# A new layout of the pairs in an interaction network: 11 loads a chunk, x1 sent early, all second-layer tiles in single precision

## The chip, the cores and the metric

One Trainium2 chip, and one of its cores. The metric is the device time of the whole program in microseconds (us), the median of several runs.

## The reference

A recommendation model over 1024 samples. Each looks up 32 rows of 64 numbers, one from each of 32 tables. Two interaction layers follow, both with 128 outputs, and then a small network with relu.

```python
def cin_layer(h, h0, W, b):              # h: [b, Hn, 64], h0: [b, 32, 64]
    Wr = W.reshape(128, Hn, 32)
    x = einsum('bhd,bmd,ohm->bod', h, h0, Wr) + b[None, :, None]
    return relu(x)
x1 = cin_layer(h0, h0, W1, b1)           # h0: the 32 rows
direct2 = cin_layer(x1[:, :64], h0, W2, b2)
z = sum(concat([x1[:, 64:], direct2], axis=1), axis=-1)
y = relu(relu(concat([z, dense_ctx]) @ W_top1 + b_top1) @ W_top2 + b_top2) @ W_top3
```

Layer 1 works on 32 x 32 pairs of rows, which are symmetric; layer 2 on 64 x 32 = 2048 pairs, 16 tiles of 128.

## The kernel before

A chunk is 8 samples, so N = 512 columns; there are 128 chunks in 64 pairs of chunks. Every tile has 128 partitions (pairs of rows) and 512 columns.

**GpSimd** looks up a pair of chunks at a time (L205) and stores the rows feature by feature into a table in HBM, `emb_rows`, with the first 16 features once more behind the 32 (L213), so that reads can wrap.

**SyncE** issues all loads, each 256 KB: `h0` (each feature four times), four `h0shift` tiles (features i+4k to i+4k+3), four `h0rep` tiles for layer 2 (L257), and, from x1 in SBUF, four `x1rep` tiles (L263), each of which spreads 8 partitions of x1 over 128. That is 13 a chunk. Two small loads per pair of chunks bring what layer 1 has left over, `rem_a` and `rem_b`. Its order for chunk c: h0 and shifts of c+2, the x1rep of c+1 as soon as its x1 is there, the h0rep of c+2.

**VectorE** forms the products. Layer 1: `prod1` (L375), 128x2048, with the four-fold h0 as the other factor, and the remainder (L371, L380). Layer 2: two instructions (L403) of 128x4096 for 16 tiles. Half of these tiles are split: ScalarE rounds them to `prod2hi` (L541), VectorE forms the rest, `prod2lo` (L410).

**TensorE** multiplies and adds up in PSUM. A tile in single precision is one matmul in the code and two instructions in the profile. A split tile is three fast matmuls (L472, L473, L479). Its order for chunk c: layer 1 of c+1 (L447, L448), eight tiles of layer 2 in single precision (L465), then the split ones, of which one in every second chunk stays single (L475).

**ScalarE** applies relu and sums over 64 columns, in eight pieces of 64 columns per layer and chunk (L519), each an ACTIVATE and a read of the accumulator. The pieces of layer 1 write all of x1, and the last one releases the fan-out:

```python
if not (last and s == 1):
    act.wait_ge(acc1_ready, c + 2)
    reduce_relu(acc1[1 - s], bias1, x1[1 - s], z1, c + 1, x1_ready)
product_hi(1)
```

All engines run the same `software_pipeline`: two steps by hand, a loop over pairs of chunks, two steps by hand. s is the buffer, the chunk's parity. The top network is run at the end.

Of the kernel before, what the change touches and what calls it, by code (L numbers as in the profile page):

```python
# [14 lines left out]

# [20 lines left out]

def build_dlrm(nc, a):
# [7 lines left out]
    with ctx:  # L47
# [9 lines left out]

        emb = nc.dram_tensor("emb_rows", [WRAP, ROW], fp32, kind="Internal")

# [5 lines left out]
        gathered = sb("gathered", [P, PAIR_GATHERS, D])  # L65
        w1T = sb("w1T", [P, K1, O])
        w1remT = sb("w1remT", [3 * REM, 2, O], fp32r)
        w2T = sb("w2T", [P, len(PLAIN) * NJ, O])
        w2full = sb("w2full", [P, O])
        w2hi = sb("w2hi", [P, len(SPLIT) * NJ, O], fp32r)  # L70
        w2lo = sb("w2lo", [P, len(SPLIT) * NJ, O], fp32r)
        w16hi = sb("w16hi", [P, HALF], fp32r)
        bias1 = sb("bias1", [P, 1])
        bias2 = sb("bias2", [P, 1])
        ident = sb("ident", [P, P])
        h0 = [sb(f"h0_{s}", [P, N]) for s in range(2)]
        h0shift = [sb(f"h0shift_{s}", [P, K1, N]) for s in range(2)]
# [4 lines left out]
        prod1 = [sb(f"prod1_{s}", [P, K1, N]) for s in range(2)]  # L82
        x1 = [sb(f"x1_{s}", [P, N]) for s in range(2)]
        x1rep = [sb(f"x1rep_{s}", [P, NI, N]) for s in range(2)]
        h0rep = [sb(f"h0rep_{s}", [P, NJ, N]) for s in range(2)]
        prod2 = [sb(f"prod2_{n}", [P, 2, NJ, N]) for n in range(2)]
        prod2hi = [sb(f"prod2hi_{n}", [P, NJ, N], fp32r) for n in range(len(SPLIT))]
        prod2lo = [sb(f"prod2lo_{n}", [P, NJ, N], fp32r) for n in range(len(SPLIT))]
# [3 lines left out]
        denseT = sb("denseT", [DENSE, B])  # L92
# [6 lines left out]

        hid1 = [prod2[h][:, 0, :, :] for h in range(2)]  # L100
        hid2 = [prod1[h] for h in range(2)]
# [6 lines left out]

        w1_in = sem("w1_in")
        weights_in = sem("weights_in")  # L110
# [8 lines left out]
        wt1a_zero = sem("wt1a_zero")  # L119
        ident_zero = sem("ident_zero")  # L120
        ident_ready = sem("ident_ready")
        w1_folded = sem("w1_folded")
        w2_grouped = sem("w2_grouped")
        weight_step = sem("weight_step")
        tp_filled = sem("tp_filled")
        tp_copied = sem("tp_copied")
        h0_in = [sem(f"h0_in_{s}") for s in range(2)]
        h0rep_in = [sem(f"h0rep_in_{s}") for s in range(2)]
# [4 lines left out]
        prod1_ready = sem("prod1_ready")  # L133
        prod2_ready = sem("prod2_ready")
        hi_ready = sem("hi_ready")
        lo_ready = sem("lo_ready")
        split_used = sem("split_used")
        acc1_ready = sem("acc1_ready")
        x1_ready = sem("x1_ready")
        z2_ready = sem("z2_ready")  # L140
# [7 lines left out]
        WEIGHT_DMAS = 11  # L148
        STORES = 16 * 2


        w1n = x1rep[0][:, 0:2, :].rearrange("o a n -> o (a n)")
        w2n = x1rep[1][:, :, :].rearrange("o a n -> o (a n)")
        w1fold = x1rep[0][:, 2, :]
        w16 = x1rep[0][:, 3, 0:HALF]
        w1rem = [x1rep[0][:, 3, P * (s + 1):P * (s + 1) + 3 * REM] for s in range(2)]
        w2r = prod2[0][:, 0, :, :].rearrange("o i (j hm) -> o i j hm", j=NJ)

        def four(t):
            return t.rearrange("p k o -> p (k o)")

        turns1 = [([w1fold[:, k * P:(k + 1) * P] for k in range(K1)], P, [(0, K1 * P, four(w1T[:, :, :]), None)]),
                  (w1rem, 3 * REM, [(0, 2 * P, four(w1remT[:, :, :]), None)])]
        turns2 = [([w2r[:, i, j, :] for j in range(NJ)], P,
                   [(0, NJ * P, four(w2T[:, NJ * n:NJ * (n + 1), :]), None)]) for n, i in enumerate(PLAIN)]
        for n, i in enumerate(SPLIT):
            k = NJ * n
            parts = [(0, NJ * P, four(w2hi[:, k:k + NJ, :]), four(w2lo[:, k:k + NJ, :]))]  # L170
            if n == len(SPLIT) - 1:
                parts.append(((NJ - 1) * P, NJ * P, w2full[:, :], None))
            turns2.append(([w2r[:, i, j, :] for j in range(NJ)], P, parts))
        turns2 += [([dense_n[:, 4 * h + t, :] for t in range(4)], DENSE,
                    [(0, N, denseT[:, h * N:(h + 1) * N], None)]) for h in range(2)]
# [14 lines left out]
        def _(pool):  # L190
            nc.gpsimd.memset(wt1a[0:H, :], 0.0).then_inc(wt1a_zero, 1)
# [3 lines left out]
                                    base=0, pattern=[[-1, P]], channel_multiplier=1).then_inc(ident_ready, 1)  # L195
            pool.wait_ge(idx_all_ready, 1)


            with pool.Fori(0, PAIRS) as pair:

# [10 lines left out]
                for f0, nf in ((0, F), (F, WRAP - F)):  # L211
                    dst = bass.AP(emb, f0 * ROW + at, [[ROW, nf], [PAIR_GATHERS * D, GS], [1, PAIR_GATHERS * D]])
                    pool.dma_start(dst, gathered[0:nf * GS, :, :]).then_inc(emb_stored, 16)  # L213

# [3 lines left out]
        def _(sp):  # L218

# [4 lines left out]
            sp.dma_start(w2n, a["L0_rec_W2"]).then_inc(weights_in, 16)  # L224
            sp.dma_start(bias1[:, :], a["L0_rec_b1"].rearrange("(p one) -> p one", one=1)).then_inc(weights_in, 16)
            sp.dma_start(bias2[:, :], a["L0_rec_b2"].rearrange("(p one) -> p one", one=1)).then_inc(weights_in, 16)
            sp.dma_start(dense_n[:, :, :], a["dense_ctx"].rearrange("(t p) c -> p t c", p=P)).then_inc(weights_in, 16)

            sp.dma_start(wt1a[H:P, :], a["W_top1"][0:O - H, :]).then_inc(weights_in, 16)
            sp.dma_start(wt1b[:, :], a["W_top1"][O - H:2 * O - H, :]).then_inc(weights_in, 16)  # L230
            sp.wait_ge(wt1a_zero, 1)
            sp.dma_start(wt1a[0:DENSE, :], a["W_top1"][2 * O - H:2 * O - H + DENSE, :]).then_inc(weights_in, 16)
            sp.dma_start(wt2[:, :, :], a["W_top2"].rearrange("(k p) n -> p k n", p=P)).then_inc(weights_in, 16)
            with nc.allow_non_contiguous_dma(reason="short columns of biases"):
                sp.dma_start(wt3[:, :], a["W_top3"].rearrange("(k p) one -> p (k one)", p=P)).then_inc(weights_in, 16)
                sp.dma_start(bt1[:, :], a["b_top1"].rearrange("(k p) -> p k", p=P)).then_inc(weights_in, 16)
                sp.dma_start(bt2[:, :], a["b_top2"].rearrange("(k p) -> p k", p=P)).then_inc(weights_in, 16)

            def load_h0(col, s):


                sp.dma_start(h0[s][:, :], bass.AP(emb, col, [[ROW, F], [0, SH], [1, N]])).then_inc(h0_in[s], 16)
                for k in range(K1):
                    src = bass.AP(emb, SH * k * ROW + col, [[ROW, F], [ROW, SH], [1, N]])
                    sp.dma_start(h0shift[s][:, k, :], src).then_inc(h0_in[s], 16)

            def load_rem(col):

# [4 lines left out]
            def load_h0rep(col, s):  # L253

                for j in range(NJ):
                    src = bass.AP(emb, GM * j * ROW + col, [[0, GH], [ROW, GM], [1, N]])
                    sp.dma_start(h0rep[s][:, j, :], src).then_inc(h0rep_in[s], 16)  # L257

            def replicate_x1(s):

                for i in range(NI):
                    src = x1[s][GH * i:GH * (i + 1), :].unsqueeze(1).to_broadcast([GH, GM, N])
                    sp.dma_start(x1rep[s][:, i, :], src).then_inc(x1rep_in[s], 16)  # L263
# [3 lines left out]
            load_h0(0, 0)  # L267
            load_h0(N, 1)
            load_h0rep(0, 0)
            sp.wait_ge(x1_ready, 1)  # L270
            replicate_x1(0)
            load_h0rep(N, 1)

            def step(c, pair, s, first, last):
                if not last and s == 0:

                    sp.wait_ge(emb_stored, STORES * pair + 2 * STORES)
                if first and s == 0:
                    sp.wait_ge(prod1_ready, 1)
                else:  # L280


                    sp.wait_ge(prod2_ready, 2 * c)
                if not last:
                    load_h0((c + 2) * N, s)
# [310 lines left out]
```

## Time and profile before

| what | us |
|---|---|
| time, median of 3 runs | 2406.58 |
| fastest and slowest run | 2399.23, 2408.59 |
| span of the profiled execution | 2406.1 |
| TensorE busy in it | 2185.9 |
| VectorE busy | 2029.2 |
| ScalarE busy | 1176.8 |
| data moved by DMA | 468.52 MB, 195 GB/s |

The profile records one execution. Busy time is the union of an engine's instructions; the ends of matmuls are modelled, so they overlap in the records. The chain that ended last is followed back from the last instruction, at each step to what released it.

### The profile page before, as it was taken

The numbers are of one execution on the slowest core, as the hardware profiler recorded it, in microseconds if no ns is written. First come the engines' busy times: TensorE is split into PE (matmuls) and PEld (weight loads), VectorE is DVE, ScalarE is ACT, GpSimd is POOL, SyncE is SP. The second block draws the span as 40 slices with busy tenths as digits, with TensorE's granted clock in tenths as the row PEclk, the third lists the DMA queues.
The fourth block names the chain that finished last, engine by engine and source line by source line (L and its number), as shares of the span: only waits on it lengthen the run. The fifth ranks groups of instructions, "written<-read, shape, count | busy, mean of one in ns | idle before, by whom it ended". The sixth has DMA issues, their size and how long they took to land.

```text
span 2406.1 us, 27920 instructions
## 1 busy us (share of the span) xinstructions
PE 2185.9 (91%) x6314; PEld 1173.3 (49%) x6314; DVE 2029.2 (84%) x828; ACT 1176.8 (49%) x4496; POOL 559.8 (23%) x455
## 2 busy tenths in 40 slices
PE   4999998989999999999999999999999999999998
PEld 2544444445445445445445445445445445445444
DVE  5888888888888888888888888888888888888882
ACT  1455444544554554554554554554554554554553
POOL 4544544455445445444100000000000000000000
PEclk8999999999999999999999999999999999999999
DMA  6788787778878878888877777777777777777760
GB/s 187 207 214 209 200 208 209 205 200 210 220 195 207 213 210 204 215 213 205 211 189 188 201 189 188 201 189 188 202 188 188 199 191 188 200 190 188 198 168 18
DMA packets 262777, 468.52 MB, mean 195 GB/s; under 512 B 37473, under 2 KB 37985, under 8 KB 262642
## 3 DMA queue, kind: packets, MB, share of 16 engines
q1 hardware_dynamic: 249458, 447.44, 72.6%
q0 software_dynamic: 13312, 21.00, 3.3%
q8 instruction: 3, 0.05, 0.0%
q14 instruction: 4, 0.03, 0.0%
HBM read 321.49 MB, written 12.59 MB: 139 GB/s over the span
## 4 chain that ended last, share of the span: by engine, by line
DMA 29%; DVE 25%; SPq 15%; issue 13%; ACT 12%; PE 4%; ACTq 1%; DVEq 0%; POOL 0%; POOLq 0%
DMA x1rep<-x 29%; DVE prod L403 23%; SPq L263 15%; ACT x L519 11%; ACTq L519 1%; PE acc L465 1%; DVE prod L375 1%; DVE prod2lo L410 1%; PE acc L479 0%; PE acc L472 0%; PE acc L473 0%; PE tp L503 0%; PE acc L503 0%; DVEq L402 0%; ACT prod2hi L541 0%
## 5 line engine op out<-in xcount | busy, mean ns | idle before, releaser
L403 DVE TENSOR_TENSOR prod<-h0rep,x1rep 128x4096 f32<-128x4096 f32 x256 | 1121.3, 4421 | 323.5 <-DMA x1rep<-x 293.4
L465 PE MATMUL acc<-prod,w2T 128*128 128x512 f32 x2048 | 950.9, 607 | 196.3 <-DVE prod L403 196.3
L465 PEld LDWEIGHTS acc<-prod,w2T 128*128 128x128 f32 x2048 | 369.7, 190 | 752.1 <-issue 377.1
L519 ACT ACTIVATE acc<-acc,bias 128x64 f32<-128x64 f32 x1024 | 296.1, 294 | 736.8 <-PE acc L479 584.9
L541 ACT CAST prod2hi<-prod 128x2048 fp32r<-128x2048 f32 (+1 forms) x256 | 459.6, 1795 | 248.2 <-DVE prod L403 241.2
L410 DVE TENSOR_TENSOR prod2lo<-prod,prod2hi 128x2048 fp32r<-128x2048 f32 (+1 forms) x256 | 540.0, 2150 | 0.0
L447 PE MATMUL acc<-prod,w1T 128*128 128x512 f32 x1024 | 462.4, 594 | 6.9 <-DVE prod L375 6.9
L472 PE MATMUL acc<-prod2hi,w2lo 128*128 128x512 f32 x960 | 430.9, 449 | 0.0
L205 POOL DMA_INDIRECT gathered<-in_tables,idx x256 | 402.5, 1572 | 112.4 <-issue 58.5
L473 PE MATMUL acc<-prod2hi,w2hi 128*128 128x512 f32 x960 | 378.2, 394 | 0.0
L519 ACT ACTIVATE x<-acc,bias 128x64 f32<-128x64 f32 x1024 | 305.1, 323 | 10.4 <-PE acc L448 10.4
L375 DVE TENSOR_TENSOR prod<-h0shift,h 128x2048 f32<-128x2048 f32 x128 | 291.6, 2278 | 3.5 <-DMA h0shift<-emb_rows 3.5
L447 PEld LDWEIGHTS acc<-prod,w1T 128*128 128x128 f32 x1024 | 194.6, 190 | 203.9 <-issue 192.9
L479 PE MATMUL acc<-prod2lo,w2hi 128*128 128x512 f32 x960 | 290.0, 421 | 0.0
L519 ACT ACTIVATION_READ_ACCUMULATOR x<-acc,bias (+1 forms) x1024 | 220.4, 215 | 0.0
L519 ACT ACTIVATION_READ_ACCUMULATOR acc<-acc,bias (+1 forms) x1024 | 218.3, 213 | 0.8
L472 PEld LDWEIGHTS acc<-prod2hi,w2lo 128*128 128x128 f32 x960 | 180.9, 188 | 68.2 <-issue 30.6
L479 PEld LDWEIGHTS acc<-prod2lo,w2hi 128*128 128x128 f32 x960 | 180.7, 188 | 67.6 <-issue 30.7
L473 PEld LDWEIGHTS acc<-prod2hi,w2hi 128*128 128x128 f32 x960 | 180.8, 188 | 66.8 <-issue 30.6
L525 ACT CAST rem_parts<-rem_prod 32x512 fp32r<-32x512 f32 x64 | 39.7, 621 | 210.0 <-DVE rem_prod L371 188.3
L213 POOL DMA_DIRECT2D emb_rows<-gathered x128 | 73.3, 576 | 283.0 <-DMA gathered<-in_tables,idx 282.9
L201 POOL COPY idx<-idx_all 128x4 int32 x64 | 82.8, 1294 | 213.3 <-DMA emb_rows<-gathered 209.2
(61 smaller groups left out, 430.7 us busy)
## 6 DMA issues: line engine op xcount, KB each, us to landing
h0shift<-emb_rows SPq DMA_DIRECT2D x512, 256.0 KB, 4.5
h0rep<-emb_rows SPq DMA_DIRECT2D x512, 256.0 KB
x1rep<-x SPq DMA_DIRECT2D x512, 256.0 KB
h<-emb_rows SPq DMA_DIRECT2D x128, 256.0 KB, 4.5
emb_rows<-gathered POOLq DMA_DIRECT2D x64, 128.0 KB, 3.0
gathered<-in_tables,idx POOLq DMA_INDIRECT x256
emb_rows<-gathered POOLq DMA_DIRECT2D x64, 64.0 KB, 3.2
rem_a<-emb_rows SPq DMA_DIRECT2D x64, 64.0 KB
```

Source lines behind the costliest of these rows:

```text
L205: nc.gpsimd.indirect_dma_start(out=gathered[:, g, :], out_offset=None, in_=a["tables"], in_offset=bass.IndirectOffsetOnAxis(ap=idx[:, g:g ...
L263: sp.dma_start(x1rep[s][:, i, :], src).then_inc(x1rep_in[s], 16)
L375: return nc.vector.tensor_tensor(prod1[s][:, :, :], h0shift[s][:, :, :], h0[s][:, :].unsqueeze(1).to_broadcast([P, K1, N]), ALU.mult)
L403: nc.vector.tensor_tensor(prod2[n][:, :, :, :], h0rep[s][:, :, :].unsqueeze(1).to_broadcast([P, 2, NJ, N]), x1rep[s][:, 2 * n:2 * n + 2, : ...
L410: nc.vector.tensor_tensor(prod2lo[n][:, 0:m, :], prod2[n][:, 1, 0:m, :], prod2hi[n][:, 0:m, :].bitcast(fp32), ALU.subtract).then_inc(lo_re ...
L447: nc.tensor.matmul(acc1[s][:, :], w1T[:, k, :], prod1[s][:, k, :], start=(k == 0), stop=False)
L465: nc.tensor.matmul(acc2[s][:, :], w2T[:, NJ * n + j, :], prod2[n][:, 0, j, :], start=(n == 0 and j == 0), stop=False)
L472: nc.tensor.matmul(acc2[s][:, :], w2lo[:, k, :], prod2hi[n][:, j, :], start=False, stop=False)
L473: nc.tensor.matmul(acc2[s][:, :], w2hi[:, k, :], prod2hi[n][:, j, :], start=False, stop=False)
L479: mm = nc.tensor.matmul(acc2[s][:, :], w2hi[:, k, :], prod2lo[n][:, j, :], start=False, stop=(n == 1 and j == m - 1))
L519: ins = nc.scalar.activation(out[:, cols], acc[:, cols], ACT.Relu, bias=bias[:, :], accum_out=z[:, bass.ds(c * CB + b, 1)])
L541: nc.scalar.copy(prod2hi[n][:, 0:m, :], prod2[n][:, 1, 0:m, :]).then_inc(hi_ready, 1)
```

## The change

The 2048 pairs of layer 2 are laid out as those of layer 1: a tile has x1 row i (of 32) beside features i+4k to i+4k+3, for two halves of x1 and k from 0 to 7. So the four `h0shift` tiles of layer 1, now called `near`, serve k = 0 to 3 of layer 2 as well, and four `far` tiles bring k = 4 to 7. `x1rep` has two tiles, each spreading 32 partitions of x1 over 128. A chunk has 1 + 4 + 4 + 2 = 11 loads. The stored table repeats all 32 features.

No tile is split: rounding on ScalarE and the difference on VectorE are gone, and so are the fast matmuls of layer 2. ScalarE first writes the 64 rows of x1 that layer 2 needs, in one instruction without sums, and releases the fan-out; the sums of the other 64 rows come later. `prod1` has one buffer instead of two, and so has each half of the layer-2 products. TensorE's order becomes near half, layer 1 of the next chunk, far half. The weights are brought into the new order with wide copies, and the top network's weights are loaded after the first fan-out.

```diff
             def step(c, pair, s, first, last):      # TensorE
-                if not (last and s == 1):
-                    pe.wait_ge(prod1_ready, c + 2)
-                    if not (first and s == 0):
-                        pe.wait_ge(x1_ready, c)
-                    layer1(1 - s)
                 if not first:
                     pe.wait_ge(z2_ready, c - 1)
-                for n in range(2):
-                    pe.wait_ge(prod2_ready, 2 * c + (n + 1))
...
+                layer2_near(c, s)
+                if not (last and s == 1):
+                    pe.wait_ge(p1_ready, c + 2)
+                    if not (first and s == 0):
+                        pe.wait_ge(z1_ready, c)
+                    layer1(1 - s)
+                pe.wait_ge(pfar_ready, c + 1)
+                layer2_far(s)
```

```diff
             def step(c, pair, s, first, last):      # VectorE
...
+                begun = not (first and s == 0)
+                dve.wait_ge(x1rep_in[s], 16 * A2 * pair + 16 * A2)
+                if begun:
+                    dve.wait_ge(pnear_used, c)
+                products2(pnear[:, :, :, :], near[s][:, :, :], s, K1).then_inc(pnear_ready, 1)
+                dve.wait_ge(far_in[s], 16 * K2 * pair + 16 * K2)
+                if begun:
+                    dve.wait_ge(acc2_ready, c)
+                products2(pfar[:, :, :, :], far[s][:, :, :], s, K2).then_inc(pfar_ready, 1)
+                if not last:
+                    if s == 0:
+                        remainder_products(pair + 1)
+                    dve.wait_ge(acc1_ready, c + 2)
+                    done = products1(pair + 1, s)
+                    if s == 0:
+                        done = remainder_lo(pair + 1)
+                    done.then_inc(p1_ready, 1)
```

```diff
             def step(c, pair, s, first, last):      # ScalarE
...
+                if not (last and s == 1):
+                    act.wait_ge(acc1_ready, c + 2)
+                    if begun:
+
+                        act.wait_ge(x1rep_in[1 - s], 16 * A2 * (pair + s))
+                    hidden1(1 - s)
+                if begun:
+                    direct2(c - 1, 1 - s)
+                if s == 0 and not last:
+                    remainder_hi(pair + 1)
+                if not (last and s == 1):
+                    direct1(c + 1, 1 - s)
```

```diff
             def step(c, pair, s, first, last):      # SyncE
...
+                    sp.wait_ge(pnear_ready, c + 1)
+                    load_near((c + 2) * N, s)
+                    if s == 0:
+                        load_rem((c + 2) * N)
+                if not (last and s == 1):
+
+                    sp.wait_ge(x1_ready, c + 2)
+                    if not (first and s == 0):
+                        sp.wait_ge(pfar_ready, c)
+                    replicate_x1(1 - s)
+                if not last:
+                    sp.wait_ge(pfar_ready, c + 1)
+                    load_far((c + 2) * N, s)
```

`layer2_near` and `layer2_far` are eight single-precision matmuls each into the same accumulator; `hidden1` is the one relu of 64 rows, `direct1` and `direct2` are the relus with sums.

## Rows read from the trace of the kernel before

**Rows 1.** Page, engines: busy us, share, instructions.
```profile
PE 2185.9 (91%) x6314; PEld 1173.3 (49%) x6314; DVE 2029.2 (84%) x828; ACT 1176.8 (49%) x4496; POOL 559.8 (23%) x455
```

**Rows 2.** Page, chain that ended last, shares by engine.
```profile
DMA 29%; DVE 25%; SPq 15%; issue 13%; ACT 12%; PE 4%; ACTq 1%; DVEq 0%; POOL 0%; POOLq 0%
```

**Rows 3.** Chain in order of time, one chunk: start us, us, what.
```profile
1228.90 5.87 DMA x1rep<-x
...
1234.97 4.44 DVE prod L403
```

**Rows 4.** Windows: stretch, busy of engines, PEclk, DMA share, GB/s.
```profile
1217.00:1224.00 7.00, 6.28 (x16) 2.61 (x15) 7.00 (x2) 5.09 (x23) 0.00 (x0) 1.00 0.97 301
...
1227.00:1229.00 2.00, 2.00 (x7) 0.91 (x5) 2.00 (x2) 0.19 (x1) 0.00 (x0) 1.00 0.91 101
1229.50:1231.50 2.00, 2.00 (x10) 1.62 (x9) 2.00 (x3) 1.24 (x2) 0.00 (x0) 1.00 0.90 210
...
1218.05:1236.10 18.05, 16.69 (x49) 8.90 (x48) 16.11 (x8) 9.34 (x36) 0.00 (x0) 1.00 0.77 198
2354.40:2358.40 4.00, 0.03 (x1) 0.06 (x1) 4.00 (x2) 2.62 (x17) 0.00 (x0) 1.00 0.00 0
2358.60:2361.90 3.30, 3.30 (x5) 1.22 (x5) 3.30 (x1) 1.56 (x1) 0.00 (x0) 0.50 0.00 0
```

**Rows 5.** Chain in order of time, last chunk and top network.
```profile
2342.37 2.47 ACT x L519 x16
...
2344.90 0.57 SPq L263
...
2348.11 5.61 DMA x1rep<-x
...
2358.37 8.80 PE acc L465 x16
...
2372.74 0.86 PE acc L495 x2
...
2386.48 6.87 PE acc L503 x16
```

**Rows 6.** Timeline of one chunk: start us, us, engine, line, form, count.
```profile
1215.92 1.09 PE L479 MATMUL acc<-prod2lo,w2hi 128*128 128x512 f32 x4
...
1216.84 3.60 PE L447 MATMUL acc<-prod,w1T 128*128 128x512 f32 x8
...
1217.15 0.29 ACT L519 ACTIVATE acc<-acc,bias 128x64 f32<-128x64 f32 x1 [7.54 <-PE acc L479]
...
1219.88 0.80 PE L448 MATMUL acc<-rem_parts,w1remT 96*128 96x512 f32 x1
...
1230.08 2.27 DVE L375 TENSOR_TENSOR prod<-h0shift,h 128x2048 f32<-128x2048 f32 x1
1230.18 0.62 ACT L525 CAST rem_parts<-rem_prod 32x512 fp32r<-32x512 f32 x1 [2.99 <-DVE rem_prod L371]
...
1232.37 0.68 DVE L380 TENSOR_TENSOR rem_parts<-rem_prod,rem_parts 32x512 fp32r<-32x512 f32 x1
```

**Rows 7.** Line 567, top layers' relu: duration ns min/median/max.
```profile
L567 ACT ACTIVATE prod<-acc,bt x6: 687/688/722, 2375.1 to 2393.4; 128x512 f32<-128x512 f32 x6
```

**Rows 8.** DMA issues by line: KB each, us to landing.
```profile
x1rep<-in_L_rec_W SPq DMA_DIRECT2D x1, 512.0 KB, 3.7
...
table_row<-in_table_rows SPq DMA_DIRECT2D x1, 0.5 KB, 2.4
```

**Rows 9.** Chain in order of time, while gathers run.
```profile
316.26 6.25 DMA x1rep<-x
```

**Rows 10.** Timeline of the start.
```profile
29.61 5.89 PE L447 MATMUL acc<-prod,w1T 128*128 128x512 f32 x8 [6.90 <-DVE prod L375]
...
38.28 5.36 SPq L263 DMA_DIRECT2D x1rep<-x  x4
...
52.74 7.58 PE L465 MATMUL acc<-prod,w2T 128*128 128x512 f32 x11 [13.35 <-DVE prod L403]
```

More of the change, by code:

```diff
@@ L81, in build_dlrm @@
         rem_parts = sb("rem_parts", [3 * REM, N], fp32r)
[L82 to L88, printed above, removed]
+        prod1 = sb("prod1", [P, K1, N])
+        x1 = [sb(f"x1_{s}", [H, N]) for s in range(2)]
+        x1rep = [sb(f"x1rep_{s}", [P, A2, N]) for s in range(2)]
+        pnear = sb("pnear", [P, A2, K1, N])
+        pfar = sb("pfar", [P, A2, K2, N])
         z1 = sb("z1", [P, B])
@@ L107, in build_dlrm @@
         top_acc = [acc1[0], acc1[1], tp[0], tp[1]]
+        w1n = near[1][:, 0:2, :].rearrange("o a n -> o (a n)")
+        w1rem = [near[1][:, 2, 3 * REM * u:3 * REM * (u + 1)] for u in range(2)]
+        w2n = far[1][:, :, :].rearrange("o a n -> o (a n)")
+        w1wide = prod1[:, :, :].rearrange("o a n -> o (a n)")
+        w2wide = pnear[:, :, :, :].rearrange("o a k n -> o (a k n)")
+        w2staged = pfar[:, 0, :, :]
+        w1staged = pfar[:, 1, 0, :]
+        hid1 = [pnear[:, 0, :, :], pnear[:, 1, :, :]]
+        hid2 = [prod1[:, 2 * h:2 * h + 2, :] for h in range(2)]
         w1_in = sem("w1_in")
-        weights_in = sem("weights_in")
+        w2_in = sem("w2_in")
+        small_in = sem("small_in")
+        top_in = sem("top_in")
         ids_in = sem("ids_in")
@@ L164, in build_dlrm @@
[L164 to L173, printed above, removed]
@@ L243, in load_h0, with load_near, load_far @@
+            def load_near(col, s):
+                sp.dma_start(h0[s][:, :], bass.AP(emb, col, [[ROW, F], [0, SH], [1, N]])).then_inc(near_in[s], 16)
                 for k in range(K1):
                     src = bass.AP(emb, SH * k * ROW + col, [[ROW, F], [ROW, SH], [1, N]])
-                    sp.dma_start(h0shift[s][:, k, :], src).then_inc(h0_in[s], 16)
+                    sp.dma_start(near[s][:, k, :], src).then_inc(near_in[s], 16)
+            def load_far(col, s):
+                for k in range(K2):
+                    src = bass.AP(emb, SH * (K1 + k) * ROW + col, [[ROW, F], [ROW, SH], [1, N]])
+                    sp.dma_start(far[s][:, k, :], src).then_inc(far_in[s], 16)
@@ L265, in _ @@
             sp.wait_ge(emb_stored, STORES)
             load_rem(0)
-            load_h0(0, 0)
-            load_h0(N, 1)
-            load_h0rep(0, 0)
+            load_near(0, 0)
+            load_far(0, 0)
+            sp.wait_ge(tp_copied, 2)
+            load_near(N, 1)
+            sp.wait_ge(w2_wide, 1)
+            sp.wait_ge(w2_second, 1)
+            load_far(N, 1)
             sp.wait_ge(x1_ready, 1)
             replicate_x1(0)
-            load_h0rep(N, 1)
-            def step(c, pair, s, first, last):
[L275 to L283, printed above, removed]
+            sp.wait_ge(top_zero, 1)
@@ new lines, in _ @@
+            nc.vector.tensor_copy(wide2[:, :, 0:F], w2n.rearrange("o (h m) -> o h m", m=F)).then_inc(w2_wide, 1)
+            dve.wait_ge(w2_wide, 1)
+            dve.wait_ge(w2_second, 1)
+            for h in range(A2):
+                last = nc.vector.tensor_copy(in_tiles(w2staged[:, h, :]), diagonals(w2wide, SH * K1, F * h))
+            last.then_inc(far_staged, 1)
+            dve.wait_ge(tp_filled, 1)
+            nc.vector.tensor_copy(flat(w1T[:, :, :]), tp[0][:, 0:K1 * P]).then_inc(tp_copied, 1)
@@ L369, in remainder_products @@
+            dve.wait_ge(top_zero, 1)
+            for h in range(2):
+                dve.wait_ge(tp_filled, 7 + h)
+                last = nc.vector.tensor_copy(z1[0:DENSE, h * N:(h + 1) * N], tp[h][0:DENSE, :])
+                last.then_inc(tp_copied, 1)
+            last = None
             def remainder_products(pair):
@@ L441, in _, with turn @@
[L441 to L443 removed]
+            def turn(n, sources, rows):
+                if n >= 2:
+                    pe.wait_ge(tp_copied, n - 1)
+                for k, src in enumerate(sources):
+                    mm = nc.tensor.transpose(tp[n % 2][0:rows, k * P:(k + 1) * P], src, ident[:, :])
+                mm.then_inc(tp_filled, 1)
+            pe.wait_ge(w1_staged, 1)
+            turn(0, *W1_TURN)
@@ L445, in layer1 @@
+            pe.wait_ge(w1_second, 1)
+            turn(1, *REM_TURN)
+            pe.wait_ge(far_staged, 1)
+            for h in range(A2):
+                turn(2 + h, *FAR_TURNS[h])
+            pe.wait_ge(near_staged, 1)
+            for h in range(A2):
+                turn(4 + h, *NEAR_TURNS[h])
+            pe.wait_ge(small_in, 16 * SMALL_DMAS)
+            for h in range(2):
+                turn(6 + h, *DENSE_TURNS[h])
             def layer1(s):
                 for k in range(K1):
-                    nc.tensor.matmul(acc1[s][:, :], w1T[:, k, :], prod1[s][:, k, :], start=(k == 0), stop=False)
+                    nc.tensor.matmul(acc1[s][:, :], w1T[:, k, :], prod1[:, k, :], start=(k == 0), stop=False)
@@ L448, in layer1, with layer2_far, layer2_near @@
                 nc.tensor.matmul(acc1[s][:, :], w1remT[:, s, :], rem_parts[:, :],
                                  start=False, stop=True).then_inc(acc1_ready, 1)
-            pe.wait_ge(prod1_ready, 1)
+            def layer2_far(s):
+                for t in range(T):
+                    mm = nc.tensor.matmul(acc2[s][:, :], w2T[:, t, :], pfar[:, t // K2, t % K2, :],
+                                          start=False, stop=(t == T - 1))
+                mm.then_inc(acc2_ready, 1)
+            def layer2_near(c, s):
+                pe.wait_ge(pnear_ready, c + 1)
+                for t in range(T):
+                    mm = nc.tensor.matmul(acc2[s][:, :], w2nearT[:, t, :], pnear[:, t // K1, t % K1, :],
+                                          start=(t == 0), stop=False)
+                mm.then_inc(pnear_used, 1)
@@ L452, in _ @@
+            pe.wait_ge(p1_ready, 1)
             layer1(0)
             def step(c, pair, s, first, last):
-                if not (last and s == 1):
-                    pe.wait_ge(prod1_ready, c + 2)
-                    if not (first and s == 0):
-                        pe.wait_ge(x1_ready, c)
-                    layer1(1 - s)
                 if not first:
                     pe.wait_ge(z2_ready, c - 1)
-                for n in range(2):
-                    pe.wait_ge(prod2_ready, 2 * c + (n + 1))
-                    for j in range(NJ):
-                        nc.tensor.matmul(acc2[s][:, :], w2T[:, NJ * n + j, :], prod2[n][:, 0, j, :],
-                                         start=(n == 0 and j == 0), stop=False)
@@ L530, in _ @@
             nc.scalar.activation(y[0:1, 0:1], ident[0:1, 0:1], ACT.Relu)
-            act.wait_ge(weights_in, 16 * WEIGHT_DMAS)
+            act.wait_ge(w2_in, 16)
+            nc.scalar.copy(w2wide.rearrange("o (h m) -> o h m", m=2 * F)[:, :, F:2 * F],
+                           w2n.rearrange("o (h m) -> o h m", m=F)).then_inc(w2_second, 1)
+            act.wait_ge(w2_second, 1)
+            act.wait_ge(w2_wide, 1)
+            for h in range(A2):
+                last = nc.scalar.copy(in_tiles(w2staged[:, A2 + h, :]), diagonals(w2wide, 0, F * h))
```

309 lines of the change are left out of this document (121 added, 188 removed).

## The prediction

> **What bounds the kernel now.** I read the busy line first [rows 1]: TensorE shows 91% of the span, but matmul ends are modelled, so this alone does not say that it sets the pace. The chain that ended last [rows 2] does: 29% of it is the fan-out of x1 in flight, 15% the issue of that fan-out, 25% VectorE, 12% ScalarE's relu of x1; TensorE is 4%. So a loop of waits sets the pace, and not one engine's work. Rows 3 show a chunk of it: the last of the four x1rep transfers takes 5.87 us from its issue, then the products start. One chunk takes 18.05 us [rows 4]. In it VectorE works 16.1 us and the DMA engines are 77% busy: each resource is close behind the loop, none is it.
>
> TensorE's real work per chunk comes from the chain at the end of the kernel, where every piece is exclusive [rows 5]: a single-precision matmul is two instructions in 0.86 us, and sixteen instructions are 6.87 us. A split tile costs three fast passes, each about a quarter of that, 0.23. Twelve single-precision tiles are 10.3 us, the 25 fast passes about 5.8, so some 16.1 us of 18.05 are used; the loop adds about 2.
>
> **The new order on TensorE.** This decides the case. Before, the next chunk's layer 1 runs first and the whole second layer of this chunk (about 12 us) lies behind it, as cover for relu, fan-out and products. After, one step is: near half of layer 2 for chunk c (8 tiles), layer 1 of c+1, far half of c (8 tiles), and the near half of c+1 must follow. Only the far half, 6.87 us, is cover. Everything from layer 1 to the next near products is a closed loop. Counted from the first near matmul of c:
> - near half, 8 tiles: 6.87 us [rows 5].
> - layer 1, four single-precision tiles and the remainder: 3.84 us, from 1216.84 to the end of L448 at 1220.68 [rows 6].
> - matmul end to ScalarE's start: L479 ends at 1217.01, the activation begins at 1217.15: 0.14 us [rows 6].
> - the new undivided relu of x1, 64x512 from PSUM to SBUF: no such row; the nearest is the top layers' 128x512 activation, 0.69 us [rows 7]. It replaces eight pairs, 2.47 us [rows 5], and no longer queues behind the other relu. That is the gain of sending x1 early. ScalarE to the queue: 0.03.
> - fan-out, called R: first issue to the start of the products, now two transfers of 256 KB instead of four. Worked out below: 4.5 us.
> - near products, 128x4096: 4.44 us [rows 3], and 0.06 to TensorE.
> Sum: 6.87+3.84+0.14+0.69+0.03+4.5+4.44+0.06 = 20.57 us.
>
> TensorE needs 20 tiles and one fast pass, 17.4 us. So it idles about 3.2 us in each chunk although its work grew by only 1.3.
>
> **R.** The smallest load lands 2.4 us after its issue [rows 8]. The fan-out's data add to that. Its first packets flow at 101 GB/s and later ones at 210, while loads from HBM reach 301 [rows 4]. 512 KB take 2.5 us at 210 and 1.7 at 301, so 4.1 to 4.9 in all; I take 4.5: the rate doubled when transfers from several groups of 8 source partitions were in flight together, and the new ones read 32 partitions each. Lower bound: second issue 0.64 us after the first (0.57 and the gap [rows 5]), the smallest landing 2.4, and 0.15 to the start: 3.2. Upper bound: the second lands as late behind the first as the fourth does behind three: 0.64+5.87+0.15 = 6.7. The 3.7 us of the 512 KB weight load [rows 8] lies inside.
>
> The Trainium skill (SBUF, "Door 1: The DMA port swizzle") holds that partitions 0 to 7 reach two ports, with about 54 GB/s, and 32 partitions eight, with 218. The trace shows 101 for eight partitions, about twice that. By the page's figure for 32 partitions R would be 2.4+2.4+0.15 = 4.95 and the total some 57 us above mine.
>
> **Even chunks** have a second way to the same point, since the remainder's low part now stands on VectorE just ahead of the near products. Layer 1 ends at 10.71; relu 0.83 gives 11.54; the other relu pass, 2.47 and 0.05, 14.06; two casts of 0.62 [rows 6] 15.33; VectorE's difference 0.68 and 0.05, 16.06; products 4.50: 20.56. By chance it equals the sum above; it means that a shorter R helps odd chunks alone.
>
> **What is hidden.** The far products (4.44) run beside the near and layer 1 matmuls, 10.7 us. The next layer-one products, 2.27 us [rows 6], start when layer 1 ends and finish inside R. Their five loads and the two remainder loads are issued once the near products are done and occupy the queue for about 5 us, well before x1 at 11.5; the four far loads now come behind the fan-out and have a chunk and a half to land. ScalarE loses two casts, VectorE two differences, the queue two loads a chunk: all this lay off what becomes the loop, so its removal is worth nothing. Were the far products' cover gone, they would add 4.44.
>
> **Gathers.** While lookups run, the fan-out is slower, 6.25 us [rows 9] against 5.87. They last about 1130 us, 55 chunks of the new length, at 0.4: 22 us.
>
> **Ends.** At the start, before: layer 1 begins at 29.6, x1 goes out at 38.3, the second layer starts at 52.7 [rows 10]. After, layer 1 starts about 0.7 later (the remainder difference is last) at 30.3, takes 5.9 for its single-precision tiles at the low clock and 0.2 for the rest, and ends at 36.4, relu to 37.2, R 41.7, products 46.2. Weight staging changes form; before the loads land at 27 it costs nothing, and an overrun is paid once, up to 5 us. The end: from the last chunk's first matmul to the top network 13.9 us, two halves of 6.87 and what starts them, instead of 14.4 (2358.37 to 2372.74 [rows 5]), then 33.4 as before: 47.3.
>
> Total: 46.2 + 127 x 20.57 (2612) + 22 + 47.3 = 2728 us. The profiled span of before, 2406.1, is 0.5 below the median of 2406.6, so the two scales agree and I state 2728.
>
> **Rivals.**
> A. The clock falls in each gap. Before, a gap of 4.0 us at 2354.4 to 2358.4 was followed by 3.3 us at a granted 0.50, the 1.2 GHz level [rows 4]; sixteen instructions then took 8.80 instead of 6.87 us [rows 5]. The 18.05 us chunk, idle for about 1.4 us, kept 1.00. My gap of 3.2 lies between. Each fall costs 1.93 us on the loop: 245 us, total 2973. The Trainium skill (TensorE: Matmul & The Clock Gate, "HAM oscillation") describes just that, waits for a DMA between groups of matmuls bringing the low clock back every time.
> B. The fan-out does not get faster. R = 6.7 gives 22.8 us a chunk, 2.2 x 127 = 279 more: 3007; with a gap of 5.4 us A then joins in, 3250. For it: four transfers still show 5.61 us for the last with nothing else in flight [rows 5]. Against it: only the first stretch is slow.
> C. The other side: TensorE stays fed, because x1rep lands within the far half. Then 17.4 x 127 = 2210, with the ends 2303, 4% faster. It needs the loop without R, 16.07, and R to be at most 17.4 together, so R of 1.3 us. The smallest landing of any kind is 2.4.
> D. Nothing measurable: 18.05 a chunk needs R = 2.0, also below 2.4.
>
> **How the numbers follow.** Forecast with R from 3.2 to 5.3, 2645 to 2830: 0.68. A: 0.13. B: 0.12. C: 0.03. D: 0.01. Slower but below 2640 (a shorter relu or start): 0.03. The range, 2640 to 2980, holds the first two. Half a percent, 12 us, is what a measurement of this kernel can tell. Faster 0.03, same 0.01, slower 0.96.
>
> **What would show it.** The changed profile should have a chunk of 20.6 us; the near half's first matmul waiting about 3 us for VectorE; VectorE waiting for x1rep; the x1rep part of the chain about a fifth and TensorE's near half and layer 1 together about half; the far half back to back behind layer 1. A granted clock near 0.9 means A, an x1rep trip above 6 us B. What would make the whole wrong is layer 1's result reaching the near products by a shorter way than listed.

## The result, and the profile after

The changed kernel takes 3012.07 us (median of 4 runs, 3008.53 to 3030.99) against 2407.59 for the kernel before beside it: a ratio of 1.252, with a 95% interval from 1.2469 to 1.2571. It is 25% slower; 13% was forecast, and the range ended at 2980. The profiled execution has a span of 3006.9 us.

The page: busy time, the granted clock in 40 slices, and the chain by engine and by line.

```profile
PE 2492.7 (83%) x5354; PEld 1074.7 (36%) x5354; DVE 1515.2 (50%) x538; ACT 811.7 (27%) x4371; POOL 577.8 (19%) x456
...
PEclk7898898989989889999998899999999989999899
...
PE 54%; DMA 19%; DVE 19%; ACT 3%; SPq 3%; issue 2%; POOL 0%; DVEq 0%; ACTq 0%; POOLq 0%
PE acc L451 37%; DMA x1rep<-x 19%; DVE pnear L380 19%; PE acc L438 15%; ACT x L510 3%; SPq L248 2%; PE acc L439 1%; PE tp L489 0%; PE acc L444 0%; PE acc L489 0%; DMA near<-emb_rows 0%; DVEq L388 0%; ACTq L546 0%; POOL gathered L208 0%; PE acc L495 0%
```

TensorE is busy for 2493 us, more than the 2186 of [rows 1], and the clock line is ragged. The chain's largest part is now TensorE (54%, not 4% as in [rows 2]): the near half (L451) and layer 1 (L438). The far half (L444) has 0% of it. With the fan-out (19%), the near products (19%), relu and queue, that is the closed loop of the forecast.

The chain in order of time, from one fan-out to the next but one.

```profile
2010.66 7.11 PE acc L451 x16
2017.76 3.43 PE acc L438 x8
2021.19 0.25 PE acc L439
...
2021.56 0.69 ACT x L510
...
2022.27 0.57 SPq L248
...
2022.88 4.50 DMA x1rep<-x
...
2027.50 4.44 DVE pnear L380
...
2031.98 8.83 PE acc L451 x16
```

From 2010.66 to 2031.98 is a chunk at the full clock: 21.3 us. The loop can be read down the rows: near half 7.11, layer 1 3.43 and 0.25, relu 0.69, issue to products 2022.27 to 2027.50, 5.23, near products 4.44. The next near half takes 8.83, and that chunk 23.1. Against [rows 3], the last transfer's 5.87 has become 4.50, with two transfers fewer ahead of it.

The same two near halves in the timeline, with TensorE's idle time before each in brackets.

```profile
2010.66 7.11 PE L451 MATMUL acc<-pnear,w2nearT 128*128 128x512 f32 x16 [3.71 <-DVE pnear L380]
...
2031.98 8.83 PE L451 MATMUL acc<-pnear,w2nearT 128*128 128x512 f32 x16 [3.68 <-DVE pnear L380]
```

One idle time of 3.71 us left the clock up, one of 3.68 did not. In the timeline of the whole kernel 40 of the 128 near halves take 7.1 us, 44 about 8.8 and 44 about 9.8; the median idle time before the quick ones and before the slow ones is the same, 3.71 us. Over the kernel (the groups by line: busy time, mean ns, idle time before):

```profile
L451 PE MATMUL acc<-pnear,w2nearT 128*128 128x512 f32 x2048 | 1102.2, 700 | 486.3 <-DVE pnear L380 486.3
L444 PE MATMUL acc<-pfar,w2T 128*128 128x512 f32 x2048 | 900.0, 592 | 0.0
```

The windows: two stretches of the fan-out, and what follows the gap (as in [rows 4], the columns end with granted clock, DMA share, GB/s).

```profile
2002.30:2003.30 1.00, 1.00 (x3) 0.38 (x2) 0.20 (x1) 1.00 (x9) 0.00 (x0) 1.00 0.90 106
2003.50:2005.50 2.00, 2.00 (x7) 0.80 (x6) 0.68 (x1) 1.95 (x9) 0.00 (x0) 1.00 0.97 215
2032.10:2035.10 3.00, 3.00 (x5) 1.24 (x6) 3.00 (x1) 0.00 (x0) 0.00 (x0) 0.60 0.52 154
```

After the second gap the granted clock of a 3 us stretch is 0.60, a mix of the two levels, 0.5 (1.2 GHz) and 1.0 (2.4 GHz). The fan-out's first microsecond flows at 106 GB/s and a later stretch of two at 215, much as with four transfers of 8 partitions in [rows 4] (101 and 210). The 215 are not the fan-out's alone: the far loads are issued from 2002.26 on, and from 2002.0 to 2005.5 about 590 KB flow, more than the fan-out has. The chain's first and last near half, which give the mean chunk, (2959.70 - 50.47) / 127 = 22.91 us:

```profile
50.47 10.05 PE acc L451 x16
...
2959.70 7.11 PE acc L451 x16
```

### The profile page after: what moved, and what is told of

It reads as the page before. It is cut to its first block, busy times and chain, and to the rows that moved or that the text cites. A ratio compares the mean times of both kernels' runs of the same rounds, so it can differ in the third digit from the quotient of the medians.

```text
span 3006.9 us, 24844 instructions
## 1 busy us (share of the span) xinstructions
PE 2492.7 (83%) x5354; PEld 1074.7 (36%) x5354; DVE 1515.2 (50%) x538; ACT 811.7 (27%) x4371; POOL 577.8 (19%) x456
## 4 chain that ended last, share of the span: by engine, by line
PE 54%; DMA 19%; DVE 19%; ACT 3%; SPq 3%; issue 2%; POOL 0%; DVEq 0%; ACTq 0%; POOLq 0%
PE acc L451 37%; DMA x1rep<-x 19%; DVE pnear L380 19%; PE acc L438 15%; ACT x L510 3%; SPq L248 2%; PE acc L439 1%; PE tp L489 0%; PE acc L444 0%; PE acc L489 0%; DMA near<-emb_rows 0%; DVEq L388 0%; ACTq L546 0%; POOL gathered L208 0%; PE acc L495 0%
## 5 line engine op out<-in xcount | busy, mean ns | idle before, releaser
L451 PE MATMUL acc<-pnear,w2nearT 128*128 128x512 f32 x2048 | 1102.2, 700 | 486.3 <-DVE pnear L380 486.3
L444 PE MATMUL acc<-pfar,w2T 128*128 128x512 f32 x2048 | 900.0, 592 | 0.0
L451 PEld LDWEIGHTS acc<-pnear,w2nearT 128*128 128x128 f32 x2048 | 447.7, 224 | 1140.6 <-issue 838.3
L380 DVE TENSOR_TENSOR pnear<-near,x1rep 128x4096 f32<-128x4096 f32 x128 | 566.4, 4425 | 317.3 <-DMA x1rep<-x 317.3
L365 DVE TENSOR_TENSOR prod<-near,h 128x2048 f32<-128x2048 f32 x128 | 293.5, 2293 | 774.8 <-PE acc L439 768.7
L505 ACT ACTIVATE acc<-acc,bias 128x64 f32<-128x64 f32 (+1 forms) x2048 | 580.1, 287 | 22.3 <-PE acc L444 15.8
L380 DVE TENSOR_TENSOR pfar<-far,x1rep 128x4096 f32<-128x4096 f32 x128 | 565.5, 4418 | 0.0
L444 PEld LDWEIGHTS acc<-pfar,w2T 128*128 128x128 f32 x2048 | 388.9, 190 | 465.5 <-issue 460.1
L438 PE MATMUL acc<-prod,w1T 128*128 128x512 f32 x1024 | 463.4, 595 | 14.0 <-DVE rem_parts L370 14.0
L505 ACT ACTIVATION_READ_ACCUMULATOR acc<-acc,bias (+2 forms) x2048 | 424.2, 207 | 1.5
L438 PEld LDWEIGHTS acc<-prod,w1T 128*128 128x128 f32 x1024 | 195.5, 191 | 260.5 <-issue 246.1
L439 PE MATMUL acc<-rem_parts,w1remT 96*128 96x512 f32 x128 | 102.1, 798 | 0.0
```

Source lines behind the costliest of these rows:

```text
L365: return nc.vector.tensor_tensor(prod1[:, :, :], near[s][:, :, :], h0[s][:, :].unsqueeze(1).to_broadcast([P, K1, N]), ALU.mult)
L380: return nc.vector.tensor_tensor(out, h0part.unsqueeze(1).to_broadcast([P, A2, k, N]), x1rep[s][:, :, :].unsqueeze(2).to_broadcast([P, A2, ...
L438: nc.tensor.matmul(acc1[s][:, :], w1T[:, k, :], prod1[:, k, :], start=(k == 0), stop=False)
L439: nc.tensor.matmul(acc1[s][:, :], w1remT[:, s, :], rem_parts[:, :], start=False, stop=True).then_inc(acc1_ready, 1)
L444: mm = nc.tensor.matmul(acc2[s][:, :], w2T[:, t, :], pfar[:, t // K2, t % K2, :], start=False, stop=(t == T - 1))
L451: mm = nc.tensor.matmul(acc2[s][:, :], w2nearT[:, t, :], pnear[:, t // K1, t % K1, :], start=(t == 0), stop=False)
```

## The experiments

All edits are to the changed kernel unless said otherwise. A ratio is to runs of the kernel before that were taken beside that run.

### Layer 1 first

```diff
 def step(c, pair, s, first, last):      # TensorE
-    if not first:
-        pe.wait_ge(z2_ready, c - 1)
-    layer2_near(c, s)
     if not (last and s == 1):
         ...
         layer1(1 - s)
+    if not first:
+        pe.wait_ge(z2_ready, c - 1)
+    layer2_near(c, s)
     pe.wait_ge(pfar_ready, c + 1)
     layer2_far(s)
```

> The changed kernel with one edit: on TensorE, layer 1 of the next chunk goes ahead of the near half again, as in the kernel before. Theory (the order of TensorE makes the loop): relu, fan-out and near products then have both halves of layer 2 as cover; the near products can start when the near half has freed their buffer, 6.9 us after layer 1, or when x1rep lands, 6.1 us after it, and are ready 11.4 us after layer 1, while TensorE is busy for 17.4. So TensorE never waits, a chunk takes 17.4 to 17.6 us, the granted clock is 1.00 and the time is 127 x 17.5 + 50 + 47 = about 2320 us, below both kernels. Rival (the single buffers of the products, or the fan-out itself, hold the chunk, whatever the order): a chunk stays above 20 us, 2600 us or more.

Measured: 2305.79 us, ratio to the kernel before 0.960 (0.9579 to 0.962). The chain in order of time, and the windows of one chunk:

```profile
1212.84 3.43 PE acc L438 x8
1216.27 0.23 PE acc L439
1216.50 6.87 PE acc L451 x16
1223.37 6.87 PE acc L444 x16
```

```profile
1200.00:1217.40 17.40, 17.40 (x42) 7.79 (x41) 12.41 (x5) 6.76 (x36) 9.93 (x7) 1.00 0.67 188
```

There is nothing but TensorE in the chain, 17.40 us busy of 17.40, at a clock of 1.00. One moved block turns 25% slower into 4% faster. The single buffers do cost waits on VectorE, here before the near and the far products, as the timeline shows, but they end long before TensorE asks:

```profile
1206.01 4.43 DVE L380 TENSOR_TENSOR pnear<-near,x1rep 128x4096 f32<-128x4096 f32 x1 [1.80 <-PE acc L451]
...
1212.94 4.42 DVE L380 TENSOR_TENSOR pfar<-far,x1rep 128x4096 f32<-128x4096 f32 x1 [2.51 <-PE acc L444]
```

The order was the cause of the loop; with it put right, the layout, the 11 loads, the single buffers and the work in single precision make none.

### The gap filled

```diff
     layer2_far(s)
+    for _ in range(3):
+        nc.tensor.matmul(tp[0][:, :], w2T[:, 0, :], warm_rhs, start=True, stop=True)
...
+warm_rhs = flat(w2nearT[:, 0:4, :])     # 512 columns; set once, ahead of the loop
```

> The changed kernel with three extra single-precision matmuls (2.6 us) after the far half, into a PSUM tile that nobody reads before the end; they lie in the 3.7 us in which TensorE waits for the near products, and nothing waits for them. Clock theory: in the changed kernel the granted clock falls to half in part of the gaps, and the near half then takes 8.8 us and more instead of 7.1; with the gap filled the clock stays at 1.00, a chunk takes 21.4 us and the time is 127 x 21.4 + 98 = about 2820 us. Rival (the low clock is no cause, the waits are): no change, 3010 us. If the extra matmuls were in the way: slower than 3010.

Measured: 2848.32 us, ratio 1.186 (1.1829 to 1.1883). 164 us less with more work on TensorE. The group of the near halves, then the windows, over 400 us:

```profile
L451 PE MATMUL acc<-pnear,w2nearT 128*128 128x512 f32 x2048 | 931.5, 609 | 169.8 <-DVE pnear L380 169.8
```

```profile
400.00:800.00 400.00, 373.68 (x853) 162.75 (x853) 212.49 (x73) 111.84 (x612) 222.25 (x160) 0.98 0.55 157
```

The clock is 0.98 here (the same stretch of the changed kernel has 0.91). The near halves are 171 us shorter together (931.5 against 1102.2), which is the whole gain. TensorE still waits 1.3 us a chunk for the near products, so the extra matmuls are in nobody's way. Eleven near halves are still slow, all but the first of them after gaps of 2.4 to 2.9 us. So the low clock costs the changed kernel at least 164 of its 604 us; the loop at the full clock keeps the rest.

### One extra matmul

The same edit with `range(1)`.

> The changed kernel with one extra matmul (0.86 us) after the far half instead of three, so that TensorE idles for about 2.9 us instead of 3.7. If gaps of about 3 us leave the clock alone, as the prediction took it for its 3.2: granted clock 0.98 or more and about 2850 us, as with three. If they bring it down nearly as often as those of 3.7: clock below 0.95 and 2930 us or more.

Measured: 2947.29 us, ratio 1.225. The group of the near halves and the same window:

```profile
L451 PE MATMUL acc<-pnear,w2nearT 128*128 128x512 f32 x2048 | 1032.9, 663 | 386.6 <-DVE pnear L380 386.6
```

```profile
400.00:800.00 400.00, 344.11 (x759) 148.78 (x757) 204.51 (x71) 112.14 (x612) 226.46 (x163) 0.95 0.53 153
```

The window's clock lies at 0.95, between the two expectations; the time meets the second. Gaps of about 2.8 us (3.7 less 0.86), smaller than the 3.2 of the forecast, still bring the clock down often: 68 of the 128 near halves are slow, against 88. The forecast's own gap would not have been safe.

### Far loads one step later

```diff
 def step(c, pair, s, first, last):      # SyncE
...
+    if not (first and s == 0) and not (last and s == 1):
+        sp.wait_ge(pfar_ready, c)
+        load_far((c + 1) * N, 1 - s)
     if not (last and s == 1):
         sp.wait_ge(x1_ready, c + 2)
...
-    if not last:
-        sp.wait_ge(pfar_ready, c + 1)
-        load_far((c + 2) * N, s)
```

> The changed kernel with the four far loads of a chunk issued one step later, ahead of the wait for x1 instead of right behind the x1rep transfers, so that they are not in flight beside them. Theory (far loads compete with the fan-out): issue to start of the near products falls from 5.2 to about 4.6 us, the gap with it to 3.1, the clock falls less often; 2860 to 2930 us. Rival (the fan-out's own pace sets its 5.2 us): the trip stays 5.2 us and the time within 1% of 3010 us.

Measured: 3132.03 us, ratio 1.304 (1.301 to 1.3065): both expectations missed. The chain in order of time:

```profile
2029.07 9.84 PE acc L451 x16
...
2043.41 0.57 SPq L248
...
2048.26 4.44 DVE pnear L380
```

The trip did get shorter (2043.41 to 2048.26, 4.85 us instead of 5.2), so the far loads do compete a little. But the near half shown takes 9.8 us. The group of all near halves, and the window with a granted clock of 0.85 over 400 us:

```profile
L451 PE MATMUL acc<-pnear,w2nearT 128*128 128x512 f32 x2048 | 1259.9, 785 | 453.2 <-DVE pnear L380 453.2
```

```profile
400.00:800.00 400.00, 339.33 (x683) 145.40 (x682) 197.25 (x67) 103.65 (x567) 219.40 (x166) 0.85 0.52 148
```

The gaps are 33 us shorter in sum than in the changed kernel (453.2 against 486.3), the near halves 158 us longer; the difference, 125, is the loss of 120. Of the 128 near halves 127 are slow, after a median gap of 3.49 us. A shorter gap with more falls: how often the clock falls isn't told by the gap's length alone. That it depends on how gaps and work follow each other is likely but not shown.

This run also has a fan-out with nothing else in flight (x1rep is issued at 2019.52, the products start at 2024.50). Windows of its slow start, of the two microseconds behind it, and of its whole flow:

```profile
2020.90:2021.90 1.00, 1.00 (x3) 0.38 (x2) 0.21 (x1) 1.00 (x9) 0.00 (x0) 1.00 0.91 106
2021.90:2023.90 2.00, 2.00 (x6) 0.95 (x5) 0.68 (x1) 1.95 (x8) 0.00 (x0) 1.00 0.84 197
2020.70:2024.00 3.30, 3.30 (x9) 1.50 (x8) 1.10 (x2) 3.25 (x17) 0.00 (x0) 1.00 0.83 159
```

So the slow start is the fan-out's own: 106 GB/s, then 197. Its 512 KB take 3.3 us, from 1.2 us after the first issue to 0.5 us before the products.

### Both edits

Three extra matmuls and the later far loads.

> The changed kernel with both edits: three extra matmuls after the far half, and the far loads one step later. By itself the later issue shortened x1rep's way from 5.26 to 5.00 us and yet made the kernel 4% slower, with the low clock behind every gap. Theory (that loss was the clock's alone): with the gap filled the shorter way is a gain, 0.3 x 127 = 40 us below the version with the extra matmuls alone: about 2810 us. Rival (the later far loads are late for the far products, or are in the way of others): above 2850 us.

Measured: 2822.68 us, ratio 1.173 (the same window again):

```profile
400.00:800.00 400.00, 372.19 (x862) 162.69 (x862) 216.68 (x74) 112.39 (x612) 222.12 (x140) 1.00 0.53 155
```

With the clock held up, the later loads save 26 us where alone they cost 120. The kernels before beside the two versions with extra matmuls measured 2401.73 and 2405.90, so the gain is 26 to 30. The slowdown of the experiment before this one was therefore the clock's.

### A short second transfer

```diff
 def replicate_x1(s, full=True):
     for h in range(A2):
-        src = x1[s][F * h:F * (h + 1), :].unsqueeze(1).to_broadcast([F, SH, N])
-        sp.dma_start(x1rep[s][:, h, :], src).then_inc(x1rep_in[s], 16)
+        n = N if full or h == 0 else F
+        src = x1[s][F * h:F * (h + 1), 0:n].unsqueeze(1).to_broadcast([F, SH, n])
+        sp.dma_start(x1rep[s][:, h, 0:n], src).then_inc(x1rep_in[s], 16)
...
-        replicate_x1(1 - s)
+        replicate_x1(1 - s, first and s == 0)
```

> The changed kernel, but from the second chunk on the second x1rep transfer carries 32 of its 512 columns (the other columns keep the values of the first chunks, so the second half of x1 is wrong there). Theory (bytes of the fan-out set its trip, at 210 GB/s or so): the trip falls from 5.2 by about 1.2 to 4.0 us, the gap to 2.5, the clock falls seldom or never; 2670 to 2860 us. Rival (a fixed cost or the first transfer sets the trip): no change.

Measured: 2728.79 us, ratio 1.135. The chain in order of time, an even and an odd chunk:

```profile
2018.22 0.25 PE acc L440
...
2023.59 4.44 DVE pnear L381
...
2039.77 0.57 SPq L249
...
2043.67 4.44 DVE pnear L381
```

The time lies in the range of the theory. In the second chunk, 2039.77 to 2043.67 is a trip of 3.90 us: 240 KB less save 1.3. Gaps of 2.1 to 2.9 us preceded 26 of the 33 slow near halves here. In the first chunk, x1rep is not in the chain at all: layer 1 ends at 2018.47, relu, the sums, two casts and the difference follow, and the near products start at 2023.59, 5.12 us later. That is the second way of the even chunks.

### The kernel before with layer 1 in the middle

```diff
 def step(c, pair, s, first, last):      # TensorE, kernel before
-    if not (last and s == 1):
-        ... layer1(1 - s)
     if not first:
         pe.wait_ge(z2_ready, c - 1)
     for n in range(2):                  # eight tiles in single precision
         ...
+    if not (last and s == 1):
+        ... layer1(1 - s)
     for n in range(2):                  # split tiles
```

> The kernel before with one edit: on TensorE, layer 1 of the next chunk moves from the front of the step to between the eight single-precision tiles and the split ones. Theory (the place of layer 1 makes the loop, in either layout): from the first single-precision matmul 7.8 us for those tiles (the second half waits for its products), 3.7 layer 1, 2.6 relu in pieces, 9.3 fan-out of four, 4.5 products: 28 us a chunk, 3650 us, and up to 4000 with the low clock after each gap of 10 us. Rival (the new layout and the work in single precision slowed the kernel, not the order): within 5% of 2405 us.

Measured: 3871.78 us, ratio 1.610 (2 runs). The chain in order of time:

```profile
1220.96 9.60 PE acc L460 x16
1230.56 3.43 PE acc L447 x8
1234.00 0.25 PE acc L448
...
1236.95 0.59 SPq L263
...
1246.27 4.44 DVE prod L403
1250.75 9.64 PE acc L460 x15
```

29.8 us from one group of single-precision matmuls to the next (1220.96 to 1250.75), and those take 9.6 us. The same place of layer 1 makes the same loop in the old layout. It costs more there: relu takes 2.7 us (1234.25 to 1236.95) instead of 0.8, and the fan-out of four transfers 9.3 (1236.95 to 1246.27) instead of 5.2.

### Layer 1 first, x1 sent late

```diff
 # ScalarE, in the version with layer 1 first
+    direct1(c + 1, 1 - s)
     hidden1(1 - s)
...
-    direct1(c + 1, 1 - s)
```

> The version with layer 1 first, but ScalarE sends x1 late: the eight pieces of sums first, then the one relu that releases the fan-out, 2.4 us later. Theory (with layer 1 first the whole second layer is cover): x1rep lands 9.3 us after layer 1, the near products are ready at 13.8, before TensorE wants them at 17.4: the time stays at 2306 us, within 0.5%. Rival (sending x1 early is what makes that version fast): up to 2.4 us more a chunk, 2610 us.

Measured: 2305.64 us beside 2305.79, ratios 0.959 and 0.960. Sending x1 early is worth nothing once the order gives it cover.

### Layer 1 first, four tiles split

```diff
 def layer2_far(c, s):                   # TensorE
-    for t in range(T): ... w2T[:, t, :], pfar[:, t // K2, t % K2, :]
+    for t in range(K2): ... w2T[:, t, :], pfar[:, 0, t, :]
+    pe.wait_ge(hi_ready, c + 1)
+    for t in range(K2): ... w2lo, pfarhi;  w2hi, pfarhi
+    pe.wait_ge(lo_ready, c + 1)
+    for t in range(K2): ... w2hi, pfarlo
...
+dve.wait_ge(hi_ready, c + 1)            # VectorE, last in the step
+nc.vector.tensor_tensor(pfarlo[:, :, :], pfar[:, 1, :, :], pfarhi[:, :, :].bitcast(fp32), ALU.subtract)
+act.wait_ge(pfar_ready, c + 1)          # ScalarE, after the remainder's casts
+nc.scalar.copy(pfarhi[:, :, :], pfar[:, 1, :, :])
```

> The version with layer 1 first, with four of the sixteen second-layer tiles (the far ones of the second half of x1) split again as in the kernel before: ScalarE rounds, VectorE forms the difference, TensorE makes three fast passes of 0.23 us instead of 0.86. Theory (that version is bound by TensorE alone, so passes are all that counts): 4 x (0.86 - 0.70) = 0.65 us less a chunk, 16.75 us, about 2225 us. Rival (VectorE, at 14 of 16.75 us with the differences, or ScalarE's cast becomes late and holds TensorE): 2306 us or more.

Measured: 2297.03 us, ratio 0.956 (0.9534 to 0.9583): 9 us, not 81. The chain in order of time:

```profile
1817.11 4.35 DVE pnear L393
...
1826.05 3.07 DMA rem_b<-emb_rows
...
1831.12 1.91 ACT pfarhi L576
...
1835.27 4.43 DVE pnear L393
```

TensorE is not in this stretch of the chain, and the page gives it 12% of the whole. The chain runs from the near products over the queue's issues to the landing of a remainder load, the remainder's product, ScalarE's casts, VectorE's difference (2.2 us up to 1835.27), and back to VectorE's near products. The rival came about: the split work became late.

### Four tiles split, difference early

```diff
 def step(c, pair, s, first, last):      # VectorE, against the former version
     ... far products
+    dve.wait_ge(hi_ready, c + 1)
+    ... pfarlo = pfar[:, 1] - pfarhi
     ... remainder and layer-1 products
-    dve.wait_ge(hi_ready, c + 1)
-    ... pfarlo = pfar[:, 1] - pfarhi
 def step(c, pair, s, first, last):      # ScalarE
+    act.wait_ge(pfar_ready, c + 1)
+    ... pfarhi = rounded pfar[:, 1]
     ... the remainder's casts
-    act.wait_ge(pfar_ready, c + 1)
-    ... pfarhi = rounded pfar[:, 1]
```

> The version with layer 1 first and four tiles split, with another order on two engines: VectorE forms the difference right after the far products, ahead of the layer-1 products, and ScalarE rounds ahead of the remainder's casts. The layer-1 products then no longer make the rest wait for their near loads. Theory (in the former version VectorE's waits took what TensorE had saved): VectorE needs 14.1 us of work and waits 2.4 for the cast, 16.5 a chunk, TensorE 16.75: about 2230 us. Rival (VectorE's wait for the cast, or ScalarE, is now late): 2297 us or more.

Measured: 2218.37 us, ratio 0.923 (0.9208 to 0.9245), the fastest of all. Page, engines:

```profile
PE 2183.1 (98%) x5866; PEld 1109.4 (50%) x5866; DVE 1786.6 (81%) x667; ACT 1049.3 (47%) x4499; POOL 792.7 (36%) x456
```

TensorE is busy for 98%. 87 us less than with sixteen tiles in single precision, 0.69 a chunk, against 0.65 expected. So splitting none was a cost of the change too, though a small one beside the order.

## Why the prediction was wrong

**The loop: right.** It said that only the far half covers the way from layer 1 to the near products. The chain has exactly its pieces and the first experiment removes it by the order alone. As forecast, the chain gives the near half and layer 1 about half and the fan-out a fifth. The near half, layer 1, relu and products measured 7.11, 3.68, 0.69 and 4.44 against 6.87, 3.84, 0.69 and 4.44.

**The step that failed: "My gap of 3.2 lies between", taken as one that leaves the clock up.** The sum took all matmuls at the full clock; rival A, at 0.13, was the truth for most of the gaps, 88 of 128. From the groups by line, 1102 us in 128 near halves are 8.61 us each instead of 7.11, so 1.5 us a chunk or 190 us in all. Rival A had a price of 1.93 for every gap; a fall costs 1.7 or 2.7 us here, 2.2 in the mean, and not every gap brought one. The forecast had one gap of 4.0 us with a fall and one below 2 without, and put 3.2 with the latter. The experiments show that 2.8 would not have been safe.

The Trainium skill (TensorE: Matmul & The Clock Gate, "HAM oscillation") describes this case, a wait for a DMA between groups of matmuls that brings the low clock back every time. The trace agrees in part: 0.921 mean granted clock against 0.996, but after 88 of 128 waits and not after each.

**The trip of x1, a term too small.** 5.23 instead of 4.5 us. The step behind it was that reading 32 partitions spares the slow start. It doesn't: with nothing else in flight 106 GB/s first, then 197. With 0.02 of small pieces a chunk at the full clock is 21.32 instead of 20.57, 95 us in all. The Trainium skill (SBUF — State Buffer, "Door 1: The DMA port swizzle") gives 218 GB/s for 32 partitions. The fan-out alone stays below it, at 106, then 197, and 159 over its whole flow. The trip by the page's figure, 4.95, was nearer than mine, but by two errors that cancel: with nothing else in flight the trip of 4.98 has 3.3 us of data instead of 2.4, and 1.7 besides them instead of 2.55.

Each error alone would have stayed in the range: 2728 + 190 = 2918, 2728 + 95 = 2823. The two belong together: the longer trip is also the longer gap. The range took each by itself; together they gave 3012, past its end at 2980.

**Gathers.** 22 us were allowed. What is left of the 279 us between forecast and span, after 190 for the clock, 95 for the loop and 4 for the start, is -10: by this remainder they cost some 12.

**The start: 4 us too early.** The first near half is at 50.47, not 46.2. The first store to HBM came 2.6 us later (17.84 instead of 15.21 us). The copy of the first indices on GpSimd took 1.77 us instead of 0.22, and the issues of the first two gathers 1.94 and 2.11 us instead of 1.17 and 0.97. Timelines of before, then after:

```profile
6.23 0.22 POOL L201 COPY idx<-idx_all 128x4 int32 x1 [4.17 <-DVE idx_all L309]
```

```profile
5.89 1.90 DVE L313 TENSOR_TENSOR prod<-near 128x1024 f32<-128x1024 f32 x1
6.09 1.77 POOL L204 COPY idx<-idx_all 128x4 int32 x1 [3.12 <-DVE idx_all L305]
...
20.88 0.19 POOL L204 COPY idx<-idx_all 128x4 int32 x1 [1.87 <-DMA emb_rows<-gathered]
```

It ran beside VectorE's 1.90 us addition of two operands from SBUF. The Trainium skill (SBUF — State Buffer, "SBUF: two separate sides") says that such an operation and one of GpSimd that reads SBUF exclude each other; the numbers agree (the next copy, at 20.88 with VectorE idle, takes 0.19 us), though no run here separates the two. The end was right: 2959.70 to the end of the span is 47.2, forecast 47.3.

**What was hidden stayed hidden.** The far half follows layer 1 without a wait (L444: no idle time, against 486.3 us for L451). The even chunks' second way measured 5.12 from layer 1 to the products, forecast 5.35; it showed only where x1rep came early.

**Rivals.** B did not come: 5.2, not 6.7. C's time came about only with layer 1 first, by another way than a short R: 2305.79, where 2303 was the forecast for a TensorE that is always fed.

**Left open.** Why the falls are rarer at gaps of 3.7 us than at 3.5. The timelines show in which gaps they come: in the changed kernel's later part mostly in every second one, with runs of six to eight slow near halves in between, all after gaps of 3.6 to 3.8 us. Why is not shown.

## What to carry to other kernels

In a software pipeline, write down for each produced value the work that lies between its last matmul and its first use; that, not the sum of work, is the cover for relu, transfer and products. Moving one block of layer 1 was worth 706 us here (3012 to 2306), while the earlier send was worth nothing once it was off the loop. When a forecast leaves TensorE idle in every round, price the round at both clocks, and put the longer wait and the low clock into the same case of the range.

## What the runs showed of the hardware

- Less waiting made a kernel slower. A trip 0.3 us shorter gave a mean granted clock of 0.858 instead of 0.921 and 4% more time; with the gap filled the same edit was a gain of 26 us.
- Three useless matmuls in each gap saved 5%.
- How often a gap was followed by a slow near half, in this pipeline: none of the 221 under 1.7 us (three extra matmuls), 55 of 114 between 2.7 and 3.1 (one extra), 112 of 113 between 3.1 and 3.6 (later far loads), 80 of 116 between 3.6 and 4.0 (the changed kernel).
- A copy of x1 from 32 partitions to 128 starts as slowly as one from 8: 106 and 101 GB/s.
